# Causal attention inside a fused decoder layer on one core: mask, maximum, exponential and normalisation dealt out differently over the engines

## The reference

```python
q = (queries @ Wq.T + bq).reshape(N, L, H, -1)      # N=8, L=100, H=16, 32 columns a head
k = (keys @ Wk.T + bk).reshape(N, S, H, -1)
v = (values @ Wv.T + bv).reshape(N, S, H, -1)
sm = jnp.einsum('nlhd,nshd->nlhs', q, k) / math.sqrt(D)
causal_mask = jnp.triu(jnp.ones((L, S), dtype=bool), k=1)
sm = jnp.where(causal_mask[None, :, None, :], -jnp.inf, sm)
sm = jax.nn.softmax(sm, axis=-1)
attn = jnp.einsum('nlhs,nshd->nlhd', sm, v)
return attn.reshape(N, L, H * D) @ Wo.T + bo
```

## Time and profile before

| | |
|---|---|
| runs of the kernel | 732.82, 736.06, 725.7 us (median 732.82) |
| span of the profiled execution, first to last instruction | 723.6 us |
| that span beside the fastest run shown | 2.1 us less |
| busy in the whole span | PE 89%, DVE 59%, ACT 43%, POOL 17% |
| mean granted TensorE clock | 0.951 |

### The profile page before, as it was taken

The page is one execution under the profiler, slowest core; times in us unless marked ns, Lnnn a source line. Parts: engine busy times, 40 slices in busy tenths (PEclk is TensorE's granted clock), DMA queues, the critical chain, the costliest instruction groups (busy, mean ns, idle before and its releaser), DMA issues.

```text
span 723.6 us, 10477 instructions
## 1 busy us (share of the span) xinstructions
PE 646.0 (89%) x4192; PEld 573.5 (79%) x4192; DVE 426.7 (59%) x476; ACT 312.2 (43%) x345; POOL 125.6 (17%) x95
## 2 busy tenths in 40 slices
PE   4399999999979868969999999999999999999910
PEld 3279978779967757769999899998998989989810
DVE  3764555544399975467556565565655656556526
ACT  4343533125335455606444444544445445444313
POOL 1700000002255556418100000000000000000044
PEclk9789999999989999869999999999999999999965
DMA  8941006003100001038755555655656556454035
GB/s 321 403 143 59 2 0 262 1 0 117 59 1 2 1 1 59 1 135 337 279 205 215 204 203 201 210 224 184 224 178 228 203 191 243 175 198 179 0 115 187
DMA packets 22891, 107.60 MB, mean 149 GB/s; under 512 B 3024, under 2 KB 4048, under 8 KB 12880
## 3 DMA queue, kind: packets, MB, share of 16 engines
q1 hardware_dynamic: 17632, 92.80, 35.4%
q0 software_dynamic: 3056, 10.23, 4.0%
q10 hardware_dynamic: 2176, 4.19, 1.5%
...
## 4 chain that ended last, share of the span: by engine, by line
PE 80%; DVE 9%; issue 3%; DMA 3%; ACT 2%; POOL 2%; SPq 0%; POOLq 0%; ACTq 0%; DVEq 0%
PE bank L1039 24%; PE bank L1040 24%; PE bank L1041 24%; PE bank L1074 2%; DMA x<-in_x_tok 2%; DVE probs L831 2%; PE bank L1239 2%; DVE row_sum L843 1%; PE bank L1349 1%; POOL picked L434 1%; DVE diag L737 1%; DVE row_max L837 1%; PE bank L1364 1%; PE bank L1272 1%; DMA picked<-expert_out,row 1%
## 5 line engine op out<-in xcount | busy, mean ns | idle before, releaser
L963 DVE TENSOR_TENSOR wlo<-raw,whi 128x2048 fp32r<-128x2048 f32 x64 | 146.4, 2288 | 80.8 <-ACT whi L625 77.0
L625 ACT ACTIVATE whi<-raw 128x2048 fp32r<-128x2048 f32 x64 | 122.4, 1914 | 53.9 <-PE bank L1041 49.1
L1039 PE MATMUL bank<-xg_hi,whi 128*128 128x256 f32 x512 | 145.0, 283 | 0.5 <-DVE xg_lo L970 0.5
L1041 PE MATMUL bank<-xg_hi,wlo 128*128 128x256 f32 x512 | 144.9, 283 | 0.0
L1040 PE MATMUL bank<-xg_lo,whi 128*128 128x256 f32 x512 | 144.9, 283 | 0.0
L1039 PE MATMUL bank<-whi,h_hi 128*128 128x512 f32 x256 | 100.6, 393 | 0.0
L1040 PE MATMUL bank<-wlo,h_hi 128*128 128x512 f32 x256 | 99.9, 390 | 0.0
L1041 PE MATMUL bank<-whi,h_lo 128*128 128x512 f32 x256 | 99.7, 389 | 0.0
L1039 PEld LDWEIGHTS bank<-xg_hi,whi 128*128 128x128 f32 x512 | 98.2, 192 | 1.7 <-DVE xg_lo L970 0.7
L1040 PEld LDWEIGHTS bank<-xg_lo,whi 128*128 128x128 f32 x512 | 98.2, 192 | 0.9
L1041 PEld LDWEIGHTS bank<-xg_hi,wlo 128*128 128x128 f32 x512 | 98.2, 192 | 0.0
...
...
## 6 DMA issues: line engine op xcount, KB each, us to landing
...
```

Of the source, the lines that this page charges most:

```text
L625: act.activation(whi[i % RING][:], raw[i % RING][:], ACT.Copy).then_inc(w_hi, 1)
L963: dve.tensor_tensor(wlo[i % RING][:], raw[i % RING][:], f(whi[i % RING][:]), ALU.subtract)\
L1039: pe.matmul(o, a[0], b[0], start=first, stop=False)
L1041: return pe.matmul(o, a[1], b[0], start=False, stop=last)
```

## The change

Scores, mask and softmax of an image are computed the same way mathematically, with the work dealt out differently:

- The scale 1/sqrt(32) moves from the exponential into q: ACT applies it as it moves q out of PSUM, and DVE scales the column `bq_col` once. DVE also makes two 100x100 copies, `ident_r` and `causal_r`. Three small DVE instructions, after the last L813; the first q row on ACT waits for `bq_scaled`.
- PE writes the mask into each score bank with a 400-column matmul of `ident_r` and `causal_r`, and the scores accumulate on it: four more matmuls an image, and the wait of a half is now for `s_exp`, the exponentials of the image before.
- DVE no longer copies the scores; it reads the maximum out of PSUM, negated (`minus_max`). It no longer multiplies by the reciprocal either.
- ACT takes the exponential straight from PSUM, one instruction a head with that head's negated maximum as its bias: 16 of 100 columns in place of two of 800.
- POOL no longer subtracts; it does both multiplications.
- The hand-written orders of ACT, DVE and PE change. On ACT the exponentials between the two copies of image n are now those of image n+1; they were those of image n+2. The output weights' high half stands ahead of both copies of image 5; it stood between them.

```diff
--- before.py
+++ after.py
@@ -44,7 +44,8 @@
 BLOCKS = PASSES * E
 RING = 4
 EPS = 1e-5
-MASKED = -1e30
+SCALE = float(AD) ** -0.5
+MASKED = -2.0 ** 100
 
 
 V0, U0, U1, V1, O0, O1, WK, CTX0, CTX1, WQ, WV, WO = range(12)
@@ -106,6 +107,8 @@
     x1_lo = sb("x1_lo", [P, KD, T], F32R, region_c + FEAT)
     att_hi = sb("att_hi", [P, KD, T], F32R, region_c)
     att_lo = sb("att_lo", [P, KD, T], F32R, region_c + FEAT)
+    ident_r = sb("ident_r", [L, L], F32R, region_c + 2 * FEAT)
+    causal_r = sb("causal_r", [L, L], F32R, region_c + 2 * FEAT + P * 4)
 
     moe_top = [region_a]
 
...
@@ -219,8 +222,8 @@
     kq_mm, kq_done = sem("kq_mm"), sem("kq_done")
     res2 = sem("res2")
     va_mm, va_done = sem("va_mm"), sem("va_done")
-    s_mm, s_read, s_max, s_sub, s_exp, s_total = (sem(s) for s in
-                                                ("s_mm", "s_read", "s_max", "s_sub", "s_exp", "s_total"))
+    bq_scaled, mask_ready, s_mm, s_max, s_exp, s_total = (sem(s) for s in
+                                               ("bq_scaled", "mask_ready", "s_mm", "s_max", "s_exp", "s_total"))
     s_norm = [sem(f"s_norm{r}") for r in range(2)]
     pt_mm, pt_done, pv_mm = sem("pt_mm"), sem("pt_done"), sem("pv_mm")
     at_hi, at_lo = sem("at_hi"), sem("at_lo")
@@ -386,13 +389,10 @@
 
             for n in range(N):
                 for r in range(2):
-                    pool.wait_ge(s_max, 2 * n + r + 1)
+                    pool.wait_ge(s_total, 2 * n + r + 1)
                     s = heads8(probs, n, r)
-                    pool.tensor_tensor(s, s, bc(row_max[:, n % 2, 8 * r:8 * r + 8].unsqueeze(2), [L, 8, L]),
-                                       ALU.subtract).then_inc(s_sub, 1)
-                pool.wait_ge(s_total, n + 1)
-                pool.tensor_tensor(s, s, bc(row_sum[:, n % 2, 8:16].unsqueeze(2), [L, 8, L]), ALU.mult)\
-                    .then_inc(s_norm[1], 1)
+                    pool.tensor_tensor(s, s, bc(row_sum[:, n % 2, 8 * r:8 * r + 8].unsqueeze(2), [L, 8, L]), ALU.mult)\
+                        .then_inc(s_norm[r], 1)
 
 
             pool.wait_ge(w_lo, WO)
@@ -529,7 +529,10 @@
                 if c:
                     to = q_feat[:, j, :].rearrange("p (n l) -> p n l", n=N)[:, :, hf * L // 2:(hf + 1) * L // 2]
                     frm = frm.rearrange("p (l n) -> p n l", n=N)
-                act.activation(to, frm, ACT.Identity, bias=(bq_col if c else bk_col)[:, j:j + 1])\
+                if i == 8:
+                    act.wait_ge(bq_scaled, 1)
+                act.activation(to, frm, ACT.Identity, bias=(bq_col if c else bk_col)[:, j:j + 1],
+                               scale=SCALE if c else 1.0)\
                    .then_inc(kq_done, 1)
 
             for i in range(8):
@@ -547,9 +550,17 @@
                 kq(i)
 
             def exp_of(n, r):
-                act.wait_ge(s_sub, 2 * n + r + 1)
-                act.activation(heads8(probs, n, r), heads8(probs, n, r), ACT.Exp, scale=float(AD) ** -0.5)\
-                   .then_inc(s_exp, 1)
+
+                act.wait_ge(s_max, 2 * n + r + 1)
+                if n >= 2:
+                    act.wait_ge(pt_mm, 2 * n + r - 3)
+                for j in range(2):
+                    for g in range(G4):
+                        h = (2 * r + j) * G4 + g
+                        ins = act.activation(probs[:, n % 2, h * L:(h + 1) * L],
+                                             bank[0:L, 2 * r + j, g * L:(g + 1) * L], ACT.Exp,
+                                             bias=minus_max[:, n % 2, h:h + 1])
+                ins.then_inc(s_exp, 1)
 
             def turned(n, r):
                 act.wait_ge(pt_mm, 2 * n + r + 1)
@@ -566,17 +577,13 @@
 
             exp_of(0, 0)
             exp_of(0, 1)
-            turned(0, 0)
-            exp_of(1, 0)
-            exp_of(1, 1)
             for n in range(N):
+                turned(n, 0)
+                if n + 1 < N:
+                    exp_of(n + 1, 0)
+                    exp_of(n + 1, 1)
                 turned(n, 1)
                 attended_hi(n)
-                if n + 1 < N:
-                    turned(n + 1, 0)
-                if n + 2 < N:
-                    exp_of(n + 2, 0)
-                    exp_of(n + 2, 1)
                 if n == N // 2:
                     split_hi(WO)
             split_hi(FIRST)
@@ -813,6 +820,9 @@
                 dve.tensor_tensor(x1_lo[:, :, t * P:t * P + r],
                                   bank[:, 4 + t % 2, :].rearrange("p (k c) -> p k c", k=KD)[:, :, 0:r],
                                   f(x1_hi[:, :, t * P:t * P + r]), ALU.subtract).then_inc(x1t_lo, 1)
+            dve.tensor_copy(ident_r[:], ident[0:L, 0:L])
+            dve.tensor_scalar(bq_col[:], bq_col[:], SCALE, None, ALU.mult).then_inc(bq_scaled, 1)
+            dve.tensor_copy(causal_r[:], causal[:]).then_inc(mask_ready, 1)
             split_lo(WV)
             dve.wait_ge(bias2_in, 16)
 
@@ -823,30 +833,19 @@
                 dve.tensor_tensor(v_att[:, n % 2, :], bank[0:L, 6, :], att_bias[0:L, 0, :], ALU.add)\
                    .then_inc(va_done, 1)
 
-            def scores_masked(n, r):
+            def scores_max(n, r):
+
+                m = minus_max[:, n % 2, 8 * r:8 * r + 8]
                 dve.wait_ge(s_mm, 2 * n + r + 1)
-                if n >= 2:
-                    dve.wait_ge(pt_mm, 2 * n + r - 3)
-                s = probs[:, n % 2, r * HB:(r + 1) * HB].rearrange("l (j g s) -> l j g s", j=2, g=G4)
-                dve.tensor_tensor(s, bank[0:L, 2 * r:2 * r + 2, 0:G4 * L].rearrange("l j (g s) -> l j g s", g=G4),
-                                  bc(causal[:].unsqueeze(1).unsqueeze(1), [L, 2, G4, L]), ALU.add)\
-                   .then_inc(s_read, 1)
-
-            def scores_max(n, r):
-                dve.wait_ge(s_read, 2 * n + r + 1)
-                dve.tensor_reduce(row_max[:, n % 2, 8 * r:8 * r + 8], heads8(probs, n, r), AX, ALU.max)\
-                   .then_inc(s_max, 1)
-
-            def normalised(n, r):
+                dve.tensor_reduce(m.rearrange("l (j g) -> l j g", j=2),
+                                  bank[0:L, 2 * r:2 * r + 2, 0:G4 * L].rearrange("l j (g s) -> l j g s", g=G4),
+                                  AX, ALU.max, negate=True).then_inc(s_max, 1)
+
+            def totals(n, r):
                 total = row_sum[:, n % 2, 8 * r:8 * r + 8]
                 dve.wait_ge(s_exp, 2 * n + r + 1)
                 link(dve.tensor_reduce(total, heads8(probs, n, r), AX, ALU.add))
-                if r:
-                    dve.reciprocal(total, total).then_inc(s_total, 1)
-                else:
-                    link(dve.reciprocal(total, total))
-                    dve.tensor_tensor(heads8(probs, n, r), heads8(probs, n, r), bc(total.unsqueeze(2), [L, 8, L]),
-                                      ALU.mult).then_inc(s_norm[0], 1)
+                dve.reciprocal(total, total).then_inc(s_total, 1)
 
             def attended_lo(n):
                 dve.wait_ge(at_hi, n + 1)
@@ -854,31 +853,27 @@
                 dve.tensor_tensor(mine(att_lo), bank[:, 7, 0:KD * L].rearrange("p (k c) -> p k c", k=KD),
                                   f(mine(att_hi)), ALU.subtract).then_inc(at_lo, 1)
 
-            scores_masked(0, 0)
-            scores_max(0, 0)
-            scores_masked(0, 1)
-            scores_max(0, 1)
+            for r in range(2):
+                scores_max(0, r)
             values_biased(0)
-            scores_masked(1, 0)
-            normalised(0, 0)
-            normalised(0, 1)
-            scores_masked(1, 1)
-            scores_max(1, 0)
-            scores_max(1, 1)
+            for r in range(2):
+                totals(0, r)
+            for r in range(2):
+                scores_max(1, r)
             values_biased(1)
-            normalised(1, 0)
-            normalised(1, 1)
             for n in range(N):
+                if n:
+                    attended_lo(n - 1)
+                if n + 1 < N:
+                    totals(n + 1, 0)
+                if n and n + 1 < N:
+                    values_biased(n + 1)
+                if n + 1 < N:
+                    totals(n + 1, 1)
                 if n + 2 < N:
-                    scores_masked(n + 2, 0)
                     scores_max(n + 2, 0)
-                    scores_masked(n + 2, 1)
                     scores_max(n + 2, 1)
-                attended_lo(n)
-                if n + 2 < N:
-                    normalised(n + 2, 0)
-                    values_biased(n + 2)
-                    normalised(n + 2, 1)
+            attended_lo(N - 1)
             dve.wait_ge(res2, 2)
             for t in range(TILES):
                 r = rows(t)
@@ -1206,12 +1201,15 @@
                 cols = slice(n * L, (n + 1) * L)
                 for r in range(2):
                     if n >= 1:
-                        pe.wait_ge(s_read, 2 * n + r - 1)
+                        pe.wait_ge(s_exp, 2 * n + r - 1)
+                    for j in range(2 * r, 2 * r + 2):
```

(7 more changed lines are left out.)

4 lines of the change are left out of this document (2 added, 2 removed).

## The result

The changed kernel takes 749.57 us (median of four runs, 743.7 to 752.9) against 733.29 before (725.7 to 736.1): a ratio of 1.0209, 95% interval 1.0166 to 1.0251. The forecast was 741, "within 2%"; the time lies inside the range of 728 to 753, and the measured 2.1% cannot be told from 2%. The loss, 16.3 us between the medians, is twice the 7.8 forecast.

The account below looks back on a forecast made before the run. DVE bounds the kernel before, PE 1 us behind; after the change a circle of ACT and PE does. Terms 2.2 + 0.5 + 2.3 + 1.3 + 1.5 = 7.8 us on the median 732.8 give 741, range 728 to 753.

Parts of the forecast that it names:

- DVE's relief: Attention: DVE falls from 8.33 to 5.4 us an image, but PE's 8.4 lets at most 0.15 an image return.
- The new loop: Middle images: a circle of ACT's exponentials and PE's scores and weighting takes 9.01 us, 0.46 longer than 8.55.
- my upper bound of 0.38: ACT's 100-column exponentials: 0.35 us each, one starting every 0.25; at most 0.38, without overlap.
- I take 0.08 a change: PE's switches between full and 32-row matmuls: 0.08 us each, two a half, within bounds of 0 and 0.34.
- The q stop: Before the attention: PE stops 0.9 to 2.2 us as q waits for DVE's scaled bias behind POOL; 2.2 taken.
- Image 0, +0.5: Start of scores to end of image 0's weighting: 20.4 us against 19.9, clock left up.
- Images 1 to 5, +2.3: These images take 5 x 9.01 + 1.80 = 46.85 us against 44.6, with no PE pause over 2 us.
- Image 6, +2.8: Image 6: 8.5 us against 7.2, +1.3, and +1.5 for its weighting at the lower clock after a 2 us wait.
- Image 7, 0: Image 7 and what follows: the same instructions in the same order, so no change.
- the forecast alone: Whole kernel without the rivals: 735 to 746 us, chance 0.55.
- exponentials at full duration: Rival: ACT's exponentials do not overlap, 0.35 to 0.38 us each, 10.5 to 14 us more, 751 to 755; chance 0.10.
- a low clock in every image: Rival "the clock": pauses slow PE in every image, each weighting 1.5 us more, 10.5 in all, 751; chance 0.06.

Follow-up runs that it names:

- before + masks only: The kernel before with only the mask matmuls and accumulating scores added on PE, DVE still adding its mask; ratio to before 1.0060 (1.0005 to 1.0115).
- the product on POOL alone: The kernel before with POOL doing the product with the reciprocals for both halves instead of DVE sharing it; ratio to before 0.9911 (0.9863 to 0.9958).
- scale early: The changed kernel with the q bias scaled on DVE where the constants are made, ahead of POOL's large operation; ratio to before 1.0152 (1.0069 to 1.0235).
- pauses filled: The changed kernel with unread 100x100 identity matmuls put into PE's pauses of images 0, 5, 6 and 7; ratio to before 1.0151 (1.0018 to 1.0284).
- high half moved: The kernel before with both products on POOL and the output weights' high half just ahead of image 4's split on ACT; ratios to before 0.9837, again 0.9871.
- one exponential a half: The changed kernel with one 800-column exponential a half instead of eight of 100, head 0's bias for all; ratio to before 1.0122 (1.0005 to 1.0240).
- heads only: The kernel before with exponentials head by head in SBUF, negated maximum as bias, scale in q, no POOL subtraction; ratio to before 1.0176 (1.0067 to 1.0284).

## Why the prediction was right and wrong

- **That DVE's relief would return nothing: right.** PE's work stood 1 us behind DVE. The masks alone use that up (before + masks only, 8.87); the product on POOL alone returns it (7.53).
- **The new loop, 9.01: right in size (8.93).** It is made of slightly cheaper exponentials (3.87 for 4.10) and dearer masks and scores in the second half (1.42 for 1.22). That the exponentials came so near is luck in part: one is shown with 0.40, above my upper bound of 0.38, and they overlap by 0.17, where I had 0.35 and 0.10. What I had not seen is that PE's own work, at 8.87, is nearly as long: I had 8.4. The step at fault is "I take 0.08 a change". The price is 0.43 for each further run of 32-row matmuls plus 0.17 for parting the masks. The 1.49 us less the 0.72 that I had for the masks leave 0.19 for each of four changes, inside my bounds of 0 and 0.34 and over twice the 0.08. The Trainium skill (TensorEngine Tiling (Array Packing), Key Properties) says that a change of mode drains the engine, without a price. The trace agrees in that each further run has a cost of its own, though no run parts a drain from other costs of starting one. It made no difference to the interval, since the circle is longer still.
- **The q stop, 2.2: right as a stop** (2.20). With the low clock behind it the scores started 3.5 us later than before, 4.4 later than with the scale early. My sum had no term for that clock.
- **Image 0, +0.5: wrong.** Its weighting ended at 220.63 + 3.56 = 224.2, 24.5 us after the start, against 19.9 before: +4.6. The step was "PE's idle is in pieces of about 1.0, so I leave the clock up". The pieces came as laid out (waits of 1.02 and 0.92, rows below), and PE was at 0.54 from 215 to 219 and at 0.50 until 229.
- **Images 1 to 5, +2.3: wrong, +6.2** (274.95 - 224.19 = 50.8 against 44.6). Image 1 began at the low clock (11.1 instead of 8.9), and image 5, whose pause I had called spread and so harmless, took 12.8 instead of 10.8 with its weighting at 3.56.
- **Image 6, +2.8: too much,** +1.9: PE waited 1.81 ahead of its weighting, and this took 2.13, not the 3.5 that I had added 1.5 for. The clock fell only behind it.
- **Image 7, 0: wrong,** +2.9. The instructions are the same, and the clock is not: 0.50 from 283.6 to the projection.

The stage term is then 4.6 + 6.2 + 1.9 + 2.9 = 15.6 and the q stop 3.5, together 19.1 in these two profiles, where the forecast had 7.8. The medians of the runs lie 16.3 apart. That is more than the 14.7 us at which the prediction calls itself wrong, and 749.6 lies outside the 735 to 746 that it gave for the forecast alone. The whole range held because it reached to 753 for two rivals, exponentials at full duration and a low clock in every image, and neither is what happened. So the mechanism of the middle was right, the total was inside the range partly by luck, and the failed step is the rule that I drew from three rows, that a pause of 1 us is harmless and one of over 2 us is not. I priced each weighting by the pause right in front of it. PE in image 0 of the changed kernel:

```profile
213.83 0.87 PE L1222 MATMUL bank<-ident,probs 100*100 100x100 f32 x8 [1.02 <-ACT probs_t L569]
215.62 0.98 PE L1206 MATMUL bank<-causal_r,ident_r 100*100 100x400 f32 x2 [0.92 <-ACT probs L560]
220.63 3.56 PE L1237 MATMUL bank<-probs_t,v_att 100*32 100x100 f32 x32
```

The clock fell behind pauses of about 1 us and stayed down through the work after them. The kernel before showed already that the pause in front of a weighting does not decide. In its image 0 the scores ahead of the 2.36 us pause took 1.76 instead of 1.40, so the clock was down before that pause began:

```profile
207.58 0.89 PE L1224 MATMUL bank<-ident,probs 100*100 100x100 f32 x8 [1.84 <-POOL probs L394]
208.40 1.76 PE L1213 MATMUL bank<-k_feat,q_feat 32*100 32x100 f32 x32
```

What the runs do not give is a better rule: pauses of 0.21 and 0.38 were followed by the low clock in image 0 and not in image 5 (pauses filled), and one kernel ran image 7 at either clock behind the same pauses (high half moved). The rival "the clock" had this price (10.5) but for every image of the middle, where it is wrong, and at 0.06.

Shown by experiment: that the exponentials in series make the loss (one exponential a half takes the stage from 94.8 to 79.1; heads only, without the rest of the change, loses 1.8% and 9.4 of the 15.6 us), and that a good part of it is the low clock (pauses filled; over half in that pair of profiles). Not tested by itself is the distance of one image, with the score banks held until the exponentials are done; what share it and the masks have in the other 6.2 us is open. Not settled: what exactly decides when the clock falls. A stop of 2.2 us before q was followed by a low stretch in the changed kernel, and not in the one without masks. Nor is it known why the kernel with one exponential a half ran at 732 and at 743 on the same chip.
